# A plane's own term written into the banks by ScalarE, and tiles of six classes dealt out in turn

## The reference, cut to what matters

```python
# x: (16, 512, 64, 64) fp32
x = x + _L0_conv_ref(_gn(x), ...)      # layer 0: 1x1 convolution and a 5x5 descriptor, relu
x = x + _L1_conv_ref(_gn(x), w1, b1, w2, b2)

def _L1_conv_ref(x, w1, b1, w2, b2):   # layer 1
    gap = jnp.mean(x, axis=(2, 3))
    hmid = jax.nn.relu(jnp.einsum('bc,ec->be', gap, w1) + b1)
    s = jax.nn.relu(jnp.einsum('be,ce->bc', hmid, w2) + b2)
    q_s = clip(floor(s), 0, 5); q_b = q_s + 1
    pools = stack of max pools of x with windows 1, 3, 5, 7, 9, 11, 13
    s_out, b_out = pools[q_s], pools[q_b]        # one pair per plane (b, c)
    return frac_b * b_out + frac_s * s_out + x   # frac_b = s - q_s, frac_s = q_b - s
```

## Time and profile before

| | us |
|---|---|
| median of 3 runs | 4232.78 (4231.58 to 4235.63) |
| the profiled execution, own time | 4233.84 |
| its span, first to last instruction | 4231.6 |
| PE, DVE busy | 3852.2, 3378.1 (91%, 80%) |
| ACT, POOL busy | 1679.9, 1949.9 (40%, 46%) |
| mean granted TensorE clock | 0.964 |

### The profile page before, as it was taken

How to read it: one execution, slowest core, us unless ns; L and a number is a source line. 1 busy time by engine, 2 the same in 40 slices (tenths; PEclk the granted TensorE clock), 3 DMA queues, 4 the chain that set the end, 5 groups by cost and what they waited for, 6 DMA issues and landing times. The chain is left out here.

```text
span 4231.6 us, 74174 instructions
## 1 busy us (share of the span) xinstructions
PE 3852.2 (91%) x23656; PEld 2158.0 (51%) x23657; DVE 3378.1 (80%) x3619; ACT 1679.9 (40%) x2835; POOL 1949.9 (46%) x1576
## 2 busy tenths in 40 slices
PE   4999999999999999999999993989899998888785
PEld 3666665666566566666666653333344333333332
DVE  5777777777777777777777666899988899999994
ACT  3445445545444454454445430432233222222222
POOL 3545555555555555555555541443333333333331
PEclk9999999999999999999999995999999999999888
DMA  5445454455355455445545334654477666655551
GB/s 192 155 164 176 156 176 164 165 175 183 138 181 179 141 179 177 158 162 177 181 143 181 125 117 101 240 216 180 187 279 306 245 248 258 255 239 200 219 204 74
DMA packets 252396, 782.84 MB, mean 185 GB/s; under 512 B 98151, under 2 KB 98151, under 8 KB 229991
## 3 DMA queue, kind: packets, MB, share of 16 engines
q1 hardware_dynamic: 219600, 417.85, 28.6%
q0 software_dynamic: 32288, 358.95, 21.4%
HBM read 428.22 MB, written 409.08 MB: 198 GB/s over the span
## 5 line engine op out<-in xcount | busy, mean ns | idle before, releaser
L1025 DVE TENSOR_TENSOR arena<-arena 128x2048 f32<-128x2048 f32 (+9 forms) x635 | 1454.8, 2319 | 105.6 <-PE psum L1380 49.3
L438 POOL TENSOR_TENSOR arena<-arena 128x512 f16<-128x512 f32 x512 | 648.4, 1271 | 864.0 <-ACT arena L581 862.8
L666 ACT ACTIVATE arena<-psum,arena 128x512 f32<-128x512 f32 x536 | 367.4, 687 | 1084.2 <-PE psum L1380 1080.5
L447 POOL TENSOR_TENSOR arena<-arena 128x512 f32 (+1 forms) x512 | 639.8, 1271 | 299.2 <-ACT arena L593 293.5
L1205 PE MATMUL psum<-arena 128*128 128x512 f16 x2048 | 776.1, 379 | 1.0 <-ACT arena L593 1.0
L1207 PE MATMUL psum<-arena 128*128 128x512 f16 x2048 | 776.2, 379 | 0.0
L1206 PE MATMUL psum<-arena 128*128 128x512 f16 x2048 | 776.2, 379 | 0.0
L1376 PE MATMUL psum<-arena 128*128 128x512 f32 x1072 | 580.1, 624 | 207.4 <-issue 189.4
L1182 PE MATMUL psum<-arena 128*128 128x256 f16 (+1 forms) x6344 | 718.6, 271 | 34.1 <-DVE arena L775 21.2
L579 ACT ACTIVATE arena<-arena,gbias,grstd 128x512 f32 (+1 forms) x512 | 413.6, 808 | 631.5 <-PE psum L1207 515.7
L1182 PEld LDWEIGHTS psum<-arena 128*128 128x128 f16 x6344 | 592.4, 99 | 121.3 <-DVE arena L775 28.6
(11 more groups left out here) (150 smaller groups left out, 3358.3 us busy)
## 6 DMA issues: line engine op xcount, KB each, us to landing
arena<-in_x SPq DMA_DIRECT2D x64, 2048.0 KB, 13.1
wide_planes<-arena SPq DMA_DIRECT2D x128, 1024.0 KB, 8.9
y_planes<-arena SPq DMA_DIRECT2D x64, 2048.0 KB, 7.7
arena<-arena SPq DMA_DIRECT2D x1536, 8.0 KB, 1.8
arena<-wide_planes,arena POOLq DMA_INDIRECT x72
arena<-plane_records,arena POOLq DMA_INDIRECT x67, 8.0
arena<-y_planes,arena POOLq DMA_INDIRECT x67, 10.4
out<-arena POOLq DMA_INDIRECT x67, 8.4
```

The costliest lines, as they stand in the source:

```text
L438: pool.tensor_tensor(gl[:, ct, slot], g32[:, ct % 2, :], gh[:, ct, slot], ALU.subtract).then_inc(s_gl, 1)
L447: pool.tensor_tensor(y, y, relu[:, o % 2, :], ALU.add).then_inc(s_added, 1)
L1025: ins = dve.tensor_tensor(dst, a, b, ALU.max)
```

## The change

Three things change. ScalarE gets a new function, first_terms: when the eight banks of t-1 are evicted it writes number times plane plus constant of tile t into each of the eight banks and counts s_first up. TensorE then adds only small and big (class 0: only big) onto what is there, each bank after its s_first; for this the banks are opened once by eight matmuls ahead of the first tile (s_opened). The evictions are plain copies, two diagonals are built instead of three, and the constant's copy goes. Third, the iota that fills tnum is dealt: place t does logical tile t // 6 + 12 * (t % 6). Everything that reads tnum follows: which planes go where, and the class of each place. The empty logical tiles 67 to 71 come to the places 47, 53, 59, 65 and 71.

```diff
@@ -228,10 +228,9 @@
-        diag = v(2 * 3 * P).rearrange("p (s k n) -> p s k n", s=2, k=3)
+        diag = v(2 * 2 * P).rearrange("p (s k n) -> p s k n", s=2, k=2)
...
-        const_t = v(2)
@@ -485,7 +486,10 @@
-            pool.iota(tnum_i, [[1, NT]], base=0, channel_multiplier=0).then_inc(s_iota, 1)
+            pool.iota(tnum_i.rearrange("p (b a) -> p b a", a=NCLS), [[1, NT // NCLS], [NT // NCLS, NCLS]], base=0,
+                      channel_multiplier=0).then_inc(s_iota, 1)
@@ -651,10 +655,22 @@
-                for k in range(3):
-                    act.activation(diag[:, s, k, :], ident, ACT.Copy, scale=recs_in[:, u, k:k + 1])
-                act.activation(const_t[:, s:s + 1], recs_in[:, u, 3:4], ACT.Copy).then_inc(s_diag, 1)
-
+                for k in range(2):
+                    ins = act.activation(diag[:, s, k, :], ident, ACT.Copy, scale=recs_in[:, u, k + 1:k + 2])
+                ins.then_inc(s_diag, 1)
+
+            def first_terms(t, u):
+
+                if not (isinstance(t, int) and t == 0):
+                    act.wait_ge(s_res, t * 8)
+                with act.If(class_of(t) < NCLS):
+                    for b in range(8):
+                        act.activation(psum[:, b, :], bufs[:, u, b * CW:(b + 1) * CW], ACT.Identity,
+                                       bias=recs_in[:, u, 3:4], scale=recs_in[:, u, 0:1]).then_inc(s_first, 1)
+                with act.Else():
+                    act.sem_inc(s_first, 8)
+
+                act.wait_ge(s_first, (t + 1) * 8)
                 act.wait_ge(s_diag, t + 1)
                 act.activation(recs_in[:, u, :], ident[:, 0:REC], ACT.Copy, scale=0.0)
 
@@ -663,8 +679,7 @@
-                        act.activation(bufs[:, u, b * CW:(b + 1) * CW], psum[:, b, :], ACT.Identity,
-                                       bias=const_t[:, u % 2:u % 2 + 1]).then_inc(s_res, 1)
+                        act.activation(bufs[:, u, b * CW:(b + 1) * CW], psum[:, b, :], ACT.Copy).then_inc(s_res, 1)
@@ -683,11 +698,13 @@
                     results(t - 1, (u - 1) % BUFS)
+                first_terms(t, u)
                 if not (isinstance(t, int) and t + 1 >= NT):
                     diagonals(t + 1, (u + 1) % BUFS)
 
             act.wait_ge(s_sorted, 1)
             diagonals(0, 0)
+            act.wait_ge(s_opened, 1)
@@ -1370,17 +1387,20 @@
                 for b in range(8):
-                    if not (isinstance(t, int) and t == 0):
-                        pe.wait_ge(s_res, (t - 1) * 8 + b + 1)
+                    pe.wait_ge(s_first, t * 8 + b + 1)
                     dst = psum[:, b, :]
-                    pe.matmul(dst, diag[:, s, 0, :], bufs[:, u, b * CW:(b + 1) * CW], start=True, stop=False)
                     if with_small:
-                        pe.matmul(dst, diag[:, s, 1, :], small[:, s, b * ROWS:(b + 1) * ROWS, 1:W + 1],
-                                  start=False, stop=False)
-                    pe.matmul(dst, diag[:, s, 2, :], big[:, s, b * CW:(b + 1) * CW], start=False, stop=True)\
-                      .then_inc(s_mix, 1)
+                        pe.matmul(dst, diag[:, s, 0, :], small[:, s, b * ROWS:(b + 1) * ROWS, 1:W + 1],
+                                  start=False, stop=False, skip_group_check=True)
+                    pe.matmul(dst, diag[:, s, 1, :], big[:, s, b * CW:(b + 1) * CW], start=False, stop=True,
+                              skip_group_check=True).then_inc(s_mix, 1)
 
             pe.wait_ge(s_sorted, 1)
+
+
+            for b in range(8):
+                last = pe.matmul(psum[:, b, :], ident, cst[:, 0:CW], start=True, stop=True)
+            last.then_inc(s_opened, 1)
```

More of the change, by code:

```diff
@@ L302, in build @@
         s_mix = sem("s_mix")
+        s_first = sem("s_first")
+        s_opened = sem("s_opened")
         s_res = sem("s_res")
```

## The result

The changed kernel takes **4249.33 us** (median of 7 runs, 4246.77 to 4251.13) against 4232.78 us (7 runs) of the kernel before: a ratio of 1.0036, 95% interval 1.0025 to 1.0048. It is slower by 16.5 us. Forecast were 4242, between 4222 and 4262, and slower as the likeliest sign. The profiled span is 4247.1 us, 15.5 more than before.

The account below looks back on a forecast made before the run. VectorE's pooling was taken to pace the kernel. Pooling waits rising from 76.3 to 107.7 us (+31.4), with -6.8 and -15.1 at the end, gave +9.5 on 4232.78, about 4242 us, range 4222 to 4262.

Parts of the forecast that it names:

- The bound: Second layer: VectorE's pooling paces it, 1473.9 us in 1550.2; TensorE costs only the 49.3 us that VectorE waits for it.
- release: Time from the end of VectorE's pooling of a tile until that tile is mixed: 17.4 us, entering twelve times.
- class 1 behind class 0, seven: Class 1 pooling waits for class 5 to be mixed while class 0 covers 13.87 us: 3.5 us seven times, 24.7 us.
- behind four empty tiles: VectorE stands for a full release behind empty places 47, 53, 59 and 65: 4 x 17.4 = 69.6 us.
- loads behind them: Class 1 behind tiles 48 and 54 waits for its late-issued plane: 3.9 us twice, 7.8 us.
- small steps and returns: VectorE's small steps between tiles stay 5.6 us; loop returns at 24, 36, 48 and 60 are hidden by other waits.
- last pooling to last eviction's end: End of the layer: 24.9 us becomes 17.4 + 0.7 = 18.1, a gain of 6.8 us.
- from there to the span's end: After the last eviction only the last large store and closing work remain: 32.6 us becomes 17.5, a gain of 15.1.
- First terms: ScalarE's eight per tile, 0.7 to 0.8 us each, run while TensorE waits 8 us or more for VectorE: cost 0.
- A warm TensorE: Rival: TensorE's array stays at full clock, release 15.1 us twelve times, 4215 us; chance 0.1.
- Empty tiles that cost nothing: Rival: the buffer half is free sooner, so no waits or late loads behind empty tiles, 4165 us; chance 0.05.
- Late loads behind them: Rival: late loads behind empty tiles delay evictions, stores and later loads; release 18.5, 7 us at tile 61, 4262 us; chance 0.2.

Follow-up runs that it names:

- experiment 1: Kernel before with only the own term moved to ScalarE (TensorE adds two), places in class order, not dealt: 4176.1 us, ratio 0.9868.
- experiment 8: The kernel of experiment 1 with TensorE reading the class ahead of its wait for the pools: 4174.9 us, ratio 0.9852.
- experiment 4: Changed kernel with ScalarE writing every first term twice, the second behind a wait for the first: 4252.0 us, ratio 1.0043.
- experiment 7: The kernel of experiment 6 with eleven instead of six zero-matrix products in class 5 tiles: 4208.8 us, ratio 0.9949.
- experiment 6: The kernel of experiment 5 plus six zero-matrix products on TensorE ahead of the pool wait in class 4 and 5 tiles: 4225.5 us, ratio 0.9979.
- experiment 3: Changed kernel with 66 places dealt out and logical tiles 66 to 71 in order behind them, empty tiles last: 4199.5 us, ratio 0.9917.
- experiment 2: Kernel before with only the dealt iota, TensorE still adding three terms: 4393.8 us, ratio 1.0376.
- experiment 5: Changed kernel with TensorE reading the class and branching ahead of its wait for the pools: 4232.1 us, ratio 0.9994.

## Why the prediction was right, point by point

**The bound.** VectorE's pooling paces the layer: its busy time and its times by class are the same after. Class order with a short release (experiments 1 and 8) leaves no wait of VectorE for a release.

**Term by term.** From the first pooling (2621.24) to the last (4212.64) are 1591.4 us, less 1473.9 of pooling, 117.5 us of waiting. Forecast were 107.7.

| term | forecast | measured |
|---|---|---|
| class 1 behind class 0, seven | 24.7 | 28.3 |
| behind four empty tiles | 69.6 | 73.6 |
| loads behind them | 7.8 | 6.4 |
| small steps and returns | 5.6 | 9.2 |
| last pooling to last eviction's end | 18.1 | 18.0 |
| from there to the span's end | 17.5 | 16.4 |

The places and the counts of the waits for TensorE were right. In the row of loads, luck had a part: two waits of 3.9 us were forecast and one of 3.57 came, the other was 0.73, and 2.10 us at tile 61, which the sum had at nothing (0 to 7 in its bounds), make up for much of it. The mechanism stood; what was mis-sized is the **release**, 17.4 us in the forecast. Behind the eleven waits it is 17.7 to 19.7 us, 18.4 in the mean. TensorE, class 5 tile 17, whose pooling ended at 3029.56:

```profile
3031.77 2.07 PE L1393 MATMUL psum<-arena 128*128 128x512 f32 x2 [11.62 <-issue]
3033.63 1.91 PE L1395 MATMUL psum<-arena 128*128 128x512 f32 x2
3035.34 1.65 PE L1393 MATMUL psum<-arena 128*128 128x512 f32 x2
3036.83 1.02 PE L1395 MATMUL psum<-arena 128*128 128x512 f32 x2
```

Its first matmul starts 2.2 us behind the pooling, where 1.3 us lay between them at tile 0 before. The first three pairs took 5.06 us, against 4.81, and behind the pooling of tile 64 four pairs were slow (2.07, 1.92, 1.91 and 1.39 us). In these two tiles the beginning is colder than in tile 0, on which the forecast rested, though TensorE had stood idle for 11.62 and 12.52 us instead of 28.58. But over the twelve releases the slow pairs cost 2.3 us in the mean, as in tile 0. What is longer in the mean is the start: the first matmul comes 1.35 to 2.2 us behind the pooling, 1.85 in the mean, which is 0.6 of the 1.0 us by which a release is longer; the other 0.4 stay open. The other error is in the small terms. The returns at places 24 and 36 did not disappear in the waits of the next class 1 (2.0 us together). And a tile that waits for nothing still starts some 0.15 us behind the last; the forecast carried over the 5.6 us of before, while the tiles without a wait ahead of them rose from 37 to 50.

**The closing.** 16.4 us against 17.5: the last large store is issued 1.5 us behind the last eviction, as forecast.

```profile
4203.47 5.72 ACT L668 ACTIVATE psum<-arena 128x512 f32<-128x512 f32 x8 [0.64 <-ACT arena L682]
...
4230.08 0.60 ACT L682 ACTIVATE arena<-psum 128x512 f32<-128x512 f32 x1 [1.12 <-PE psum L1395]
```

```profile
4232.15 0.99 POOL L533 DMA_INDIRECT out<-arena  x1 [23.03 <-issue]
4233.60 0.55 POOL L538 DMA_DIRECT2D no_out<-arena  x1 [0.46 <-issue]
```

**First terms.** Forecast 0.7 to 0.8 us each and free. The row of the line, with minimum, median and maximum in ns:

```profile
L668 ACT ACTIVATE psum<-arena x536: 758/765/783, 2622.2 to 4208.4; 128x512 f32<-128x512 f32 x179
```

Free by experiment 4. The eight of the last tile end 3.4 us ahead of its pooling's end (4203.47 + 5.72 against 4212.64), as the cover in the forecast asked for. TensorE waited for a first term in seven class 0 tiles, as forecast, and also in the third tile of every round (class 2, in the last round class 3), which the forecast had not: 2.1 to 2.7 us of idleness each time. VectorE waited for none of these tiles.

**The rivals.** A warm TensorE was given 0.1 and did not come about by itself. Made by hand (experiment 7), it gives 19 to 23 us, with two of the twelve releases still partly cold, where 27.6 were worked out for all twelve. What the Trainium skill says (TensorE: Matmul & The Clock Gate, What's actually happening), that the array's default is the throttled state and activity releases it, agrees with the trace: in tile 17 above the granted clock is 0.50 from 3031.8 to 3035.3 us and 1.00 from 3037 to 3048 us, and its mean is 0.81 and 0.80 in the two stretches of the result. In experiment 6, 2.3 us of idleness left the beginning warm where 5.1 did not. Empty tiles that cost nothing are ruled out by experiment 3. Late loads behind them appeared, 2.1 us at tile 61, but no further wait of VectorE followed from them. The chances, case by case, add up to 0.50 for slower and 0.35 for same, not to the 0.52 and 0.33 written; that changes no reading.

**The median.** The sum was +9.5 and the measured difference +16.5. In the rows of the table, 7.6 are the waits for releases, 3.6 the small steps, less 1.4 of loads and 1.2 at the end. That makes 8.6 and so 18.1 us for the second layer. Against it stands the first layer, which ended 2.6 us earlier in the profiled execution after (first pooling 2621.24 against 2623.87) and leaves the 15.5 by which the spans differ. In the profiled executions of the experiments that begin with a class 0 tile the first pooling starts between 2614.6 and 2626.7 us, so these 2.6 us tell nothing of the change. That the miss is 7 us and not 8.6 is chance.

## What to carry to other kernels

Write down for each buffer how long it takes from "filled" to "free again", and compare that with the work that its producer has in between: where the work is longer the wait is zero, and shortening the consumer further brings nothing. An empty turn in a double-buffered pipeline is not free; it takes away the work that hid one whole release, so empty turns belong where nothing waits, at the end. Mixing items of different cost did not help here, neither with the cheaper consumer (23 us behind class order even without holes, experiments 1 and 3) nor with the dearer one (161 us behind, holes included, experiment 2). Whether it helps where the two engines are the bound for different items in turn is not shown.

## What the runs showed of the hardware that was not expected

**A register read from SBUF can take three times as long.** TensorE's read of the class, minimum, median and maximum in ns, after and before:

```profile
L1377 PEldq TENSOR_LOAD <-arena x72: 296/587/915, 2635.2 to 4222.8; - x72
```

```profile
L1360 PEldq TENSOR_LOAD <-arena x72: 297/303/904, 2637.9 to 4219.2; - x72
```

The median went from 303 to 587 ns. At tile 17 after, it took 0.88 us and stood between the end of the pooling and the first matmul. Moving it and its branches ahead of the wait (experiment 5) took 17 us out of the kernel and brought the median to 302 ns. Dealing is not what makes it long: in class order with the read behind the wait (experiment 1) the median is 301 to 312 ns in the stretches up to 3300 us and 586 to 896 in those from 3300 to 4050 us. Nor does the median tell the cost: with the terms doubled (experiment 4) it is 308 ns and the waits are no shorter. What makes a read long stays open; no run varied that alone.

**Loop returns have no fixed price.** Four returns of VectorE's loop were 10.2 us before, 0.88 to 1.08 us each in the dealt kernel where they were visible, and 3.5 to 5.4 us each in the class-ordered kernels. Fewer returns are cheaper by 15 to 19 us in two kernels (4174.9 to 4155.9 and 4169.6 to 4154.6 us), of which 14.3 and 12.2 us lie in the second layer. Why a return costs more there is open.

**Evictions without a bias are shorter.** With the bias they took 0.69 us, as plain copies they take 0.60 us (the row at 4230.08 above); a first term, from SBUF to PSUM with scale and bias, takes 765 ns.
